# Scan states copied by another engine, and an attention mask split between contraction rows and 32x32 matmuls, in a two-layer megakernel

## The reference, cut to what matters

```python
# layer 0, attention: 16 heads of DH = 8, a band of 64 tokens to each side
scores = jnp.einsum('bhid,bhjd->bhij', q, k) * scale
band = jnp.abs(idx[:, None] - idx[None, :]) <= HALF
scores = jnp.where(band[None, None], scores, neg)
attn = jax.nn.softmax(scores, axis=-1)
out = jnp.einsum('bhij,bhjd->bhid', attn, v)
...
# layer 1, state-space part: 256 channels, 16 states, one state vector per channel
def step(h, inp):
    dA_t, dBu_t, C_t = inp
    h = dA_t * h + dBu_t
    y_t = jnp.einsum('bdn,bn->bd', h, C_t)
    return (h, y_t)
_, y = jax.lax.scan(step, h0, (dA, dBu, Cm))
```

## Time and profile before

| | |
|---|---|
| median of 3 runs | 1679.41 us (1673.42 to 1681.12) |
| profiled execution, time | 1671.59 us |
| profiled execution, span | 1669.7 us |
| mean granted TensorE clock | 0.937 |
| PE busy | 1335.8 us, 80% |
| DVE busy | 1199.0 us, 72% |
| ACT busy | 749.9 us, 45% |
| POOL busy | 638.1 us, 38% |
| chain that ended last | PE 50%, DVE 24%, issue 10%, ACT 8%, DMA 4% |

### The profile page before, as it was taken

How to read it: one execution, slowest core, us unless ns; L and a number is a source line. 1 busy time by engine, 2 the same in 40 slices (tenths; PEclk the granted TensorE clock), 3 DMA queues, 4 the chain that set the end, 5 groups by cost and what they waited for, 6 DMA issues and landing times.

```text
span 1669.7 us, 26485 instructions
## 1 busy us (share of the span) xinstructions
PE 1335.8 (80%) x8790; PEld 826.5 (50%) x8790; DVE 1199.0 (72%) x2253; ACT 749.9 (45%) x1033; POOL 638.1 (38%) x524
## 2 busy tenths in 40 slices
PE   4599987988878888988877788979887888845564
PEld 3256655733444667634444567625444676412224
DVE  2334366458999875559999775659999874479974
ACT  3222132467657143566655143466654334243321
POOL 4000000007989140018988040029887130056523
PEclk9699999999999999999999899989999999979996
DMA  6120002014111021023110030022110030022200
GB/s 157 58 50 1 1 24 52 2 39 127 57 45 32 15 48 28 10 78 98 52 45 20 17 54 23 20 99 71 53 45 14 4 58 16 1 76 65 62 0 13
DMA packets 54753, 72.27 MB, mean 43 GB/s; under 512 B 8292, under 2 KB 25596, under 8 KB 54564
## 3 DMA queue, kind: packets, MB, share of 16 engines
q1 hardware_dynamic: 49456, 68.40, 15.5%
q10 hardware_dynamic: 5156, 2.12, 0.5%
HBM read 61.36 MB, written 9.04 MB: 42 GB/s over the span
## 4 chain that ended last, share of the span: by engine, by line
PE 50%; DVE 24%; issue 10%; ACT 8%; DMA 4%; SPq 2%; POOL 1%; ACTq 1%; DVEq 1%; POOLq 0%
PE ps L900 11%; DVE hs L1304 9%; PE ps L913 6%; PE ps L794 3%; DVE hc L1316 3%; DVE negmax L1369 3%; PE ps L1057 3%; PE ps L1073 3%; DMA ks<-parts_d 3%; PE ps L1059 3%; PE ps L971 3%; PE ps L972 2%; PE ps L1103 2%; DVE x L1290 2%; PE ps L802 2%
## 5 line engine op out<-in xcount | busy, mean ns | idle before, releaser
L468 POOL TENSOR_TENSOR dBu<-du,bs 128x512 f32<-128x512 f32 x256 | 324.9, 1274 | 256.1 <-DMA bs<-b_d 212.9
L900 PE MATMUL ps<-xnT,w1T 128*128 128x512 f32 (+1 forms) x768 | 384.9, 620 | 33.9 <-ACT sa L660 14.5
L1304 DVE TENSOR_TENSOR_SCAN hs<-ps,carry,dBu 128x512 f32<-128x512 f32 x256 | 319.7, 1265 | 23.3 <-ACT ps L668 12.0
L668 ACT ACTIVATE ps<-delta,A_s 128x512 f32<-128x512 f32 x256 | 173.3, 688 | 212.0 <-DVE hs L1304 211.4
L913 PEld LDWEIGHTS ps<-w2T,hT 128*128 128x128 f32 (+1 forms) x1536 | 195.9, 199 | 120.5 <-issue 69.0
L913 PE MATMUL ps<-w2T,hT 128*128 128x128 f32 (+1 forms) x1536 | 204.7, 285 | 46.4 <-DVE x L1290 46.4
L458 POOL TENSOR_TENSOR y<-y,hc 128x512 f32<-128x512 f32 x168 | 212.9, 1268 | 26.0 <-DVE hc L1316 26.0
L900 PEld LDWEIGHTS ps<-xnT,w1T 128*128 128x128 f32 (+1 forms) x768 | 130.9, 188 | 151.7 <-issue 114.2
L441 POOL COPY x<-x 128x1024 f32<-128x1024 f32 x4 | 4.1, 1037 | 492.5 <-DVEq L190 492.5
L1279 DVE TENSOR_TENSOR hT<-sa,ps 128x512 f32<-128x512 f32 (+1 forms) x192 | 129.3, 673 | 78.4 <-PE ps L900 56.7
L1369 DVE TENSOR_REDUCE negmax<-ps 128x4 f32<-128x1024 f32 x128 | 153.7, 1222 | 39.4 <-PE ps L972 38.3
(11 more groups left out here) (228 smaller groups left out, 1933.9 us busy)
## 6 DMA issues: line engine op xcount, KB each, us to landing
bs<-b_d SPq DMA_DIRECT2D x128, 256.0 KB, 3.3
qs<-parts_d SPq DMA_DIRECT2D x144, 64.0 KB
ks<-parts_d SPq DMA_DIRECT2D x144, 64.0 KB
parts_d<-part SPq DMA_DIRECT2D x8, 768.0 KB, 3.6
st<-in_L_ffn_w SPq DMA_DIRECT2D x16, 128.0 KB, 5.6
x_in<-in_L_attn_x SPq DMA_DIRECT2D x4, 512.0 KB, 4.2
out<-res SPq DMA_DIRECT2D x4, 512.0 KB, 3.2
st<-in_L_ffn_w SPq DMA_DIRECT2D x8, 176.0 KB, 5.9
```

Of the source, the lines that this page charges most:

```text
L468: pool.tensor_tensor(dBu[g][n_ % 2][:, :], du[:, g, tb * HALF:(tb + 1) * HALF], bs[n_ % RING][:, :], ALU.mult)\
L668: act.activation(decay_bank(g), delta[:, g, tb * HALF:(tb + 1) * HALF], ACT.Exp, scale=A_s[:, g, n_:n_ + 1]).then_inc(S["dA_r"], 1)
L900: pe.matmul(bank((2, 6)[k % 2] if gate else k % 2)[0:m, :], w1T[:, k // 3, gate * F + f0:gate * F + f0 + m], xnT[:, BAND + tb * HALF:BAND ...
L1304: dve.tensor_tensor_scan(hs[g][:, :], decay_bank(g), dBu[g][n_ % 2][:, :], carry[:, g, n_:n_ + 1], ALU.mult, ALU.add).then_inc(S["h_s"], 1)
```

## The change

The change has two parts. In **M**, `hs` gets two buffers per group, which lie in the idle tiles `x_in` and `xn0`. The DVE copy into `carry` goes. ACT copies the last column instead (`keep`), for the steps of the first half only, behind the decay of the next step. A scan of the first half starts from the constant 0.0, and a scan of the second half from `carry`. DVE waits for ACT's copy of two steps earlier, in steps 2 to 17.

In **T**, the contraction gets 8 more rows that mask the band in blocks of 32 tokens, filled by POOL and four more DMAs in setup. What is left of the mask are 32x32 triangles on the block diagonal, added for all four heads by 8 small matmuls per tile (`triangles`). The four full mask matmuls per tile go, in both passes.

```diff
 R_VALID = 9 * DH
-R_MAX = R_VALID + 1
-K_QK = R_VALID + 1
+R_BAND = R_VALID + 1
+R_MAX = R_BAND + 8
+K_QK = R_MAX
 K_ALL = R_MAX + 3
+SUB = 32
...
-            hs = [sb(f"hs{g}", [P, HALF], F32, sec) for g in range(2)]
+            hs = [[t[:, 4 * j:4 * j + 4, :].rearrange("p i d -> p (i d)") for j in range(2)] for t in (x_in, xn0)]
...
-            sp.wait_ge(S["rowset"], 3)
+            sp.wait_ge(S["rowset"], 6)
...
+                sp.dma_start(qs[s][R_BAND:R_BAND + 8, :, :], band_q[:, :].unsqueeze(1).broadcast_to([8, HPS, N])).then_inc(S["rowdma"], 16)
+                sp.dma_start(k3[R_BAND:R_BAND + 8, :, :], band_k[:, 0:NPAD].unsqueeze(1).broadcast_to([8, HPS, NPAD])).then_inc(S["rowdma"], 16)
-            sp.wait_ge(S["rowdma"], 16 * 5 * 2)
+            sp.wait_ge(S["rowdma"], 16 * 7 * 2)
...
+                def keep(t, g):
+
+                    if b1 is None or t >= NST:
+                        return
+                    act.wait_ge(S["h_s"], nth("h_s", 2 * (b1 * 2 * NST + t) + g))
+                    act.copy(carry[:, g, t:t + 1], hs[g][t % 2][:, HALF - 1:HALF]).then_inc(S["carry_r"], 1)
+
...
                         decay(n_, 0)
+                        keep(n_ - 1, 0)
                         decay(n_, 1)
+                        keep(n_ - 1, 1)
...
+            def triangles(mask, i):
+
+                for k in range(2):
+                    for b in range(0, P, SUB):
+                        o = bank(2 * (i % 2) + k)[b:b + SUB, :].rearrange("p (h j c) -> p h j c", h=2, j=2)[:, :, :, b:b + SUB]
+                        m = mask[b:b + SUB, :].rearrange("p (j c) -> p j c", j=2)[:, :, b:b + SUB].unsqueeze(1).broadcast_to([SUB, 2, 2, SUB])
+                        t = pe.matmul(o, identb[b:b + SUB, b:b + SUB], m, start=False, stop=True, skip_group_check=True)
+                return t
...
-                        pe.matmul(o, qs[s % 2][0:K_QK, h, i * P:(i + 1) * P], ks[s % 2][0:K_QK, h, i * P:(i + 2) * P], start=True, stop=False)
-                        t = pe.matmul(o, identb[:, :], mask_q[:, :], start=False, stop=True)
-                    t.then_inc(S["s1_p"], 1)
+                        pe.matmul(o, qs[s % 2][0:K_QK, h, i * P:(i + 1) * P], ks[s % 2][0:K_QK, h, i * P:(i + 2) * P], start=(h % 2 == 0), stop=True,
+                                  skip_group_check=True)
+                    triangles(mask_q, i).then_inc(S["s1_p"], 1)
...
-                            pe.matmul(o, identb[:, :], mask_k[:, :], start=True, stop=False)
                             for j in range(2):
-                                t = pe.matmul(o[:, j * P:(j + 1) * P], ks[s % 2][0:K_ALL, h, (i + j) * P:(i + j + 1) * P], q, start=False, stop=(j == 1))
-                        t.then_inc(S["s2_p"], 1)
+                                pe.matmul(o[:, j * P:(j + 1) * P], ks[s % 2][0:K_ALL, h, (i + j) * P:(i + j + 1) * P], q, start=(h % 2 + j == 0), stop=True,
+                                          skip_group_check=True)
+                        triangles(mask_k, i).then_inc(S["s2_p"], 1)
...
-                    dve.memset(carry[:, :, :], 0.0).then_inc(S["carry_r"], 1)
...
-                    dve.wait_ge(S["carry_r"], b1 * (4 * NST + 1) + 1 + (2 * t - 1 + g if t else 0))
+                    if 2 <= t <= NST + 1:
+                        dve.wait_ge(S["carry_r"], b1 * 2 * NST + 2 * (t - 2) + g + 1)
...
-                    dve.tensor_tensor_scan(hs[g][:, :], decay_bank(g), dBu[g][n_ % 2][:, :], carry[:, g, n_:n_ + 1],
+                    dve.tensor_tensor_scan(hs[g][n_ % 2][:, :], decay_bank(g), dBu[g][n_ % 2][:, :], carry[:, g, n_:n_ + 1] if tb else 0.0,
...
-                    dve.tensor_copy(carry[:, g, n_:n_ + 1], hs[g][:, HALF - 1:HALF]).then_inc(S["carry_r"], 1)
```

More of the change, by code:

```diff
@@ L166, in program @@
             ones_row = sb("ones_row", [1, NPAD], BF16, sec)
+            band_q = sb("band_q", [8, N], BF16, sec)
+            band_t = sb("band_t", [8, N], BF16, sec)
+            band_k = sb("band_k", [8, N + 2 * P], BF16, sec)
         ps = ctx.enter_context(nc.psum_tensor("ps", [P, 8, 512], F32))
@@ L434, in _, with by_sub @@
             pool.memset(rows[:, BAND + N:NPAD], NEG).then_inc(S["rowset"], 1)
+            def by_sub(v):
+                return v[:, :].rearrange("r (a c w) -> r a c w", c=8, w=SUB)
+            pool.memset(band_k[:, :], 0.0).then_inc(S["band"], 1)
+            pool.memset(band_q[:, :], NEG).then_inc(S["band"], 1)
+            pool.memset(band_t[:, :], NEG).then_inc(S["band"], 1)
+            pool.wait_ge(S["band"], 3)
+            pool.affine_select(out=by_sub(band_k), in_=by_sub(band_k), compare_op=ALU.not_equal, fill=1.0, base=0,
+                               pattern=[[0, 5], [1, 8], [0, SUB]], channel_multiplier=-1).then_inc(S["rowset"], 1)
+            pool.affine_select(out=by_sub(band_q), in_=by_sub(band_q), compare_op=ALU.is_ge, fill=0.0, base=-1,
+                               pattern=[[0, 4], [1, 8], [0, SUB]], channel_multiplier=-1).then_inc(S["band"], 1)
+            pool.affine_select(out=by_sub(band_t), in_=by_sub(band_t), compare_op=ALU.is_ge, fill=0.0, base=-5,
+                               pattern=[[0, 4], [-1, 8], [0, SUB]], channel_multiplier=1).then_inc(S["band"], 1)
+            pool.wait_ge(S["band"], 5)
+            pool.affine_select(out=by_sub(band_q), in_=by_sub(band_q), compare_op=ALU.is_ge, fill=0.0, base=3,
+                               pattern=[[0, 4], [-1, 8], [0, SUB]], channel_multiplier=1).then_inc(S["band"], 1)
+            pool.wait_ge(S["band"], 6)
+            pool.tensor_tensor(band_q[:, :], band_q[:, :], band_t[:, :], ALU.add).then_inc(S["rowset"], 2)
             for name, k in CREDIT.items():
@@ L1266, in M @@
             def M(b0, b1):
-                if b1 is not None:
-                    dve.memset(carry[:, :, :], 0.0).then_inc(S["carry_r"], 1)
                 def times_g(k):
@@ L1315, in times_c @@
                     dve.wait_ge(S["y_r"], nth("y_r", 2 * k + g))
-                    dve.tensor_tensor(hc[g][n_ % 2][:, :], hs[g][:, :], bank(4), ALU.mult).then_inc(S["hc_r"], 1)
-                    dve.tensor_copy(carry[:, g, n_:n_ + 1], hs[g][:, HALF - 1:HALF]).then_inc(S["carry_r"], 1)
+                    dve.tensor_tensor(hc[g][n_ % 2][:, :], hs[g][n_ % 2][:, :], bank(4), ALU.mult).then_inc(S["hc_r"], 1)
                 def finish(tb):
@@ L1470 @@
     "std0_r", "std1_r", "xn0_r", "xn1_r", "link0", "link1", "dBu0_r", "dBu1_r", "ln0", "ln1", "q_scale",
-    "q_round", "den_r", "g_p", "a_p", "cc_p", "settled", "section", "h_s", "st_tr", "rowset",
+    "q_round", "band", "den_r", "g_p", "a_p", "cc_p", "settled", "section", "h_s", "st_tr", "rowset",
     "pad", "rowdma", "stack_in", "x_in", "hi_r", "mid_r", "lo_r", "b_out", "part_out", "nmT_r", "mp_out", "mp_in", "pv_p",
```

## The result

The changed kernel takes 1682.41 us (median of 20 runs, 1668.94 to 1692.64), the kernel before 1673.46 us (20 runs beside it, 1655.52 to 1689.43). The ratio is 1.0063, with a 95% interval of 1.0037 to 1.0089. The change made the kernel slower by 0.6%, and the prediction of 1643 us was wrong.

The account below looks back on a forecast made before the run. DVE was taken to bound M stages, PE the second passes and DVE most first passes of T. -15.6 (M) - 21.9 (T) + 1.5 (setup) = -36.0 us, a median of 1643 us; range 1627 to 1675.

Parts of the forecast that it names:

- M, forecast -15.6: M stages: 256 column copies leave DVE at 0.065 us each, less 1 us hidden; ACT's copies cost nothing.
- Rival C: M gains nothing because POOL or the chain over ACT becomes the bound, T as forecast: 1659 us; 0.20 together with D.
- T, forecast -21.9: T stages: mask matmuls leave PE; -17.8 us in second passes, -3.6 in first pass 2, -0.5 in first pass 0.
- the 3 us set aside for ACT's evacuation: Second passes in T: ACT's evacuation of 512 columns once per pass makes ACT 0.25 us late, 12 times, +3 us.
- a lower granted clock: Sign of a wrong prediction: lower clock in T stages, where PE does the same in less time and then waits; unpriced.
- the 17.8: Second passes 0, 2 and 3 of four T stages: 96 tiles at -0.24 us, less clearing and evacuation, -17.8 us.
- the other first passes are DVE's and count nothing: T's first passes apart from first pass 2: DVE limits them, so no gain, except 0.5 us granted for first pass 0.
- First pass 2, forecast -3.6: First pass 2 with the down projection in three T stages: 24 tiles at -0.15 us each, -3.6 us.
- Setup, forecast +1.5: Setup: POOL's band work and 14 DMAs delay the first load of `x` by nothing to 4 us; +1.5 us taken.
- A: Triangles in T run singly and each waits for its weights, 0.10 us each: 1735 us; chance 0.09.
- B: Triangles in T run singly with hidden weight loads, 0.06 us each: 1689 us; chance 0.13.
- D: T gains half, as tile changes cost 0.2 us or the exponential becomes the bound: 1654 us; 0.20 together with C.

Follow-up runs that it names:

- the mask part alone: Kernel before plus only the eight band rows and the triangles in both passes, states and copies left on DVE: 1692.44 us, ratio 1.0138.
- the change with the late wait: Changed kernel with PE's wait for ACT's copy of the turned maxima moved from tile 0 to tile 4 in second passes 0 and 2: 1649.53 us, ratio 0.9886.
- the M part alone: Kernel before plus only the two state buffers and ACT's copies, with attention and setup unchanged: 1660.07 us, ratio 0.9927.

## Why the prediction was wrong, point by point

**M, forecast -15.6, measured -18.1: right.** The copies gave 14.9 of it. The constant start, which I had listed as an edit and not priced, gave the rest. ACT's copies were guessed at 0.2 us and took 0.17, hidden as said. Rival C came close in place but not in time: in the first half POOL starts 16 operations in 19.68 us without a wait (804.54 to 824.22), 9.84 for a turn, slower than DVE's 9.67; its lag is taken up by the buffers, with one turn of 9.84 in the eight.

**T, forecast -21.9, measured +21.6 in the profiled run: this is the step that failed.** The tile itself was priced well: 1.56 - 0.24 = 1.32 us forecast, 1.33 measured, and 1.65 with the full matmul that clears a bank; the 3 us set aside for ACT's evacuation did not come. What failed is that the sum multiplied this by 96 tiles at the clock of the rows of before. Its last paragraph named a lower granted clock as something that would prove it wrong, but no rival held it and it had no chance and no price. Where the clock held the sum came out: second pass 3 gave 6.5 us, against 5.9 for a third of the 17.8. At 1.2 GHz a second-pass tile takes 2.27 us, 0.71 more than before, so one of them takes back what three gained.

The edit that I costed at nothing was the one that mattered most: "the other first passes are DVE's and count nothing". They count nothing as long as a faster PE only waits longer. Here PE's work was what kept the clock up. The runs show it from both sides. With light first passes (the change, the mask part alone, triangles in first passes alone, the change with the late wait) all eight second passes 0 and 2 start at 1.2 GHz. With full masks or filler in the first passes at most two of the eight do, in the profile of every kernel that was run.

**First pass 2, forecast -3.6, measured about nothing.** A tile takes 2.33 us, before 2.34. PE's own starts say why:

```profile
1023.74 0.60 PE L1015 MATMUL ps<-ks,qs 81*128 81x256 bf16 x4
1024.27 0.29 PE L1004 MATMUL ps<-mask_q,identb 32*32 32x128 bf16 x8
1024.52 0.71 PE L1049 MATMUL ps<-wo_s,u 128*128 128x128 f32 x4
1025.07 0.83 PE L1051 MATMUL ps<-wdT,hqT 128*128 128x128 f32 x6
```

The last two groups stood like this before:

```profile
1003.40 0.61 PE L1005 MATMUL ps<-wo_s,u 128*128 128x128 f32 x4
1003.84 0.83 PE L1007 MATMUL ps<-wdT,hqT 128*128 128x128 f32 x6
```

From the triangles to the next matmul it is 0.25 us. The scores ahead take 0.53 instead of the 0.44 of four matmuls of 0.11, and the four matmuls behind take 0.55 where they took 0.44 (1003.40 to 1003.84). Together 0.25 + 0.09 + 0.11 = 0.45 us, just the price of the four masks. I had 0.12 + 0.18.

**Setup, forecast +1.5, measured +9.8 at the load of `x`.** POOL's end was bounded rightly; the path was wrong. I followed POOL, SP and the DMAs, and let nothing touch DVE. The same rounding of weights ended 5.9 us later, though it began 0.5 us earlier, because its operations ran beside POOL's, and then PE, which had idled 7.7 us for it, did its matmuls at 1.2 GHz (3.78 us where 1.98 was) and lost 3.9 more. The Trainium skill's page SBUF — State Buffer, section SBUF: two separate sides, says that VectorE and GpSimd share a pair of ports, and that an operation of one can block the other's for its whole length. This trace agrees that they hold each other up: 0.96 us became 1.9 to 2.8 for DVE's operations with two inputs in SBUF while POOL worked.

**The rivals.** A and B had the triangles run singly. They don't, though B's 1689 us lies near what was measured: a right number for a wrong reason. D did not come: the change of tiles cost 0.1 us, as taken.

**What stays open.** Which measure of PE's work the chip goes by, since the runs show only where the clock fell and what stood ahead; in the run with filler it stayed at 1.2 GHz though PE was busy 27.86 of 29.60 us. And 4 us more after the last scan, in stages that neither part touches. There the clock stays at 1.2 GHz for 37.6 us in the change (1645.6 to 1683.2) and as long in the M part alone, where it was 30.7 us before (1626.7 to 1657.4). PE is busy for 39.2 instead of 35.3 us behind the last scan, which is the size of the loss; why the clock stays low longer no run shows.

## What to carry to other kernels

Work that is taken from an engine which waits anyway is not free of consequences: here PE's spare matmuls held its clock at 2.4 GHz for the next pass. Where an edit lightens PE, look for the stretches in which it already idles, close those gaps first (moving one wait was worth more than the change, while filling the first passes with matmuls that add zeros cost more than it gave), and put the saving only where PE is the bound. In setup, an idle engine's new work can slow another that shares a path with it, so price what runs beside it.

## What the runs showed of the hardware that was not expected

- Four 32x32 matmuls on four blocks of rows and columns, all into one PSUM bank, run together: 0.07 us from the first start to the last of two such sets, and 0.003 us from one start to the next within a set (270.049 to 270.059). The Trainium skill's page TensorEngine Tiling (Array Packing), section Restrictions and Gotchas, says that different row tiles cannot use one bank at once; no such cost shows in these times.
- Going from 128-row matmuls to 32x32 tiles and back cost 0.09 and 0.11 us, by the starts in first pass 2.
- A scan of 512 columns takes 1.21 us from a constant and 1.27 from a column in memory.
- Once at 1.2 GHz, PE stayed there for 13.2 us of work without a gap (250.00 to 263.20 in the change).
